# A two-layer decoder on one core: the first self-attention rewritten with four heads side by side on row groups

## The chip, the core and the metric

The kernel runs on one core of a Trainium2 chip. A core has TensorE (PE in the profile, its weight loads PEld), VectorE (DVE), ScalarE (ACT), GpSimd (POOL) and the queue of SyncE (SP), which work side by side and wait for one another by semaphores. Matrix products go from SBUF to PSUM, which has eight banks of 512 float32 columns on 128 partitions; GpSimd works on SBUF alone in this kernel. The metric is the device time of one execution in microseconds. All arrays are float32.

## The reference

Two decoder layers work on x of shape (8, 256, 256): eight batches of 256 tokens, 256 features. Each layer is a self-attention, a cross-attention to a context of 77 tokens and a mixture of experts with two of eight experts per token. Only the self-attention of the first layer is touched here. After a layer norm it computes, with 16 heads of 16 features:

```python
qkv = (x @ W_qkv).reshape(Bx, Nx, 3, H, Dh).transpose(2, 0, 3, 1, 4)
q, k, v = (qkv[0], qkv[1], qkv[2])
allowed = jnp.abs(i - j) <= half          # half = 64, Nx = 256
attn = jnp.einsum('bhqd,bhkd->bhqk', q, k) * scale
attn = jnp.where(allowed[None, None], attn, -jnp.inf)
attn = jax.nn.softmax(attn, axis=-1)
out = jnp.einsum('bhqk,bhkd->bhqd', attn, v)
return out.transpose(0, 2, 1, 3).reshape(Bx, Nx, C) @ W_proj + b_proj
```

The result is added to x. A query sees keys at most 64 places away, so a tile of 128 queries needs 192 of the 256 keys.

## The kernel before

The stages run one after another, with a barrier of all engines between them. The first self-attention is `attention(nc, "L0a", ..., windowed=True)`; its tensors begin with `L0a_`, the cross-attentions' with `L0x_` and `L1x_`, the second self-attention's with `L1a_`, the experts' with `L0f_` and `L1f_`.

One step of this stage is one head j of one batch, 16 steps a batch. The queries of eight heads lie on the 128 partitions, and the keys of a head are kept as a copy of these 128 rows in which the rows of other heads are zero (`k_m`, written by L345, 16 copies a batch). So every product contracts over 128 rows, 16 of which count. For each of the two query tiles q, TensorE makes the scores [128 queries, 192 keys] (L814) and adds the window's mask by a second product in bfloat16 (L817). VectorE takes the negated maximum over the keys (L393), ScalarE writes `prob = exp(s - max)` and the sum of each row (L587), VectorE inverts the sum (L488), GpSimd multiplies `prob` by it (L707), TensorE transposes the normalised `prob` by four products with the identity (L833), and VectorE or ScalarE in turn copies the transposed block out of PSUM (L235, L237). After every fourth head TensorE multiplies by the values (L855): four heads side by side on groups of 32 columns of the array. The projection (L921) follows once a batch, and VectorE adds it to X (L497). The products for queries, keys and values of the next batch (L745, L778) and the transposes of its normalised tokens (L758) are spread over the steps by the table `plan`.

The order on each engine is written out by hand: within `step`, TensorE first turns head j and then makes the scores of head j + 4 (`LOOK`), so four heads are on their way at once; `prob` has four buffers (`NB`), scores and transposed blocks two PSUM banks each. The second self-attention (`attention_quads`, not touched) makes its scores at L1232 with two heads at once, each on 64 rows of the array, into banks of their own.

## Time and profile before

| | us |
|---|---|
| three runs: median (lowest to highest) | 1757.69 (1747.56 to 1760.4) |
| the profiled execution: its time | 1754.57 |
| its span | 1752.9 |
| first self-attention in it, about | 9 to 292 |
| one batch of it | 33.4 |

The profile counts time from the first instruction. The batch of 33.4 us is the distance between two starts of the projection L921. The granted clock of TensorE over the whole execution is 0.956 of full speed, and 1.00 in every window of the first self-attention. The profiled execution is 3.1 us shorter than the median.

### The profile page before, as it was taken

The numbers are of one execution on the slowest core, as the hardware profiler recorded it, in microseconds if no ns is written. First come the engines' busy times: TensorE is split into PE (matmuls) and PEld (weight loads), VectorE is DVE, ScalarE is ACT, GpSimd is POOL, SyncE is SP. The second block draws the span as 40 slices with busy tenths as digits, with TensorE's granted clock in tenths as the row PEclk, the third lists the DMA queues.
The fourth block names the chain that finished last, engine by engine and source line by source line (L and its number), as shares of the span: only waits on it lengthen the run. The fifth ranks groups of instructions, "written<-read, shape, count | busy, mean of one in ns | idle before, by whom it ended". The sixth has DMA issues, their size and how long they took to land. (4 is left out here: it accounts for less than half of the span.)

```text
span 1752.9 us, 37262 instructions
## 1 busy us (share of the span) xinstructions
PE 1576.9 (90%) x10822; PEld 1309.1 (75%) x10823; DVE 824.7 (47%) x2586; ACT 778.5 (44%) x3041; POOL 600.8 (34%) x718
## 2 busy tenths in 40 slices
PE   5999997988749999996999999999688874999997
PEld 4878775766539999995677777776476664999997
DVE  5766664677723333332544444444177762222222
ACT  3665664766512222222445445544176651333333
POOL 3444443455522222221323232323055552222222
PEclk9999999999959999998999999999799986999999
DMA  9800002011113334322000000000301111343331
GB/s 332 261 11 0 0 0 104 29 40 40 37 43 72 93 82 133 74 40 62 1 1 1 1 1 1 1 1 1 111 22 40 40 40 46 86 119 90 95 85 30
DMA packets 81041, 99.32 MB, mean 57 GB/s; under 512 B 10608, under 2 KB 73664, under 8 KB 80960
## 3 DMA queue, kind: packets, MB, share of 16 engines
q1 hardware_dynamic: 65568, 78.61, 14.1%
q0 software_dynamic: 14160, 18.52, 5.8%
q10 hardware_dynamic: 1232, 1.18, 0.2%
q8 instruction: 42, 0.69, 0.2%
q14 instruction: 39, 0.32, 0.1%
HBM read 58.54 MB, written 40.92 MB: 57 GB/s over the span
## 5 line engine op out<-in xcount | busy, mean ns | idle before, releaser
L1176 POOL TENSOR_TENSOR L1a_prob<-L1a_prob,L1a_rtot 128x1024 f32<-128x1024 f32 x64 | 121.1, 1892 | 284.1 <-DVE L1a_rtot L1056 284.1
L1533 PEld LDWEIGHTS L0f_ps_h<-L0f_rows_t,L0f_w_up 128*128 128x128 f32 x1584 | 183.6, 193 | 11.7 <-issue 10.3
L1533 PE MATMUL L0f_ps_h<-L0f_rows_t,L0f_w_up 128*128 128x128 f32 x1584 | 185.2, 277 | 7.1 <-issue 7.1
L1594 ACT ACTIVATE L1f_hid<-L1f_ps_h,L1f_b_up 128x128 f32<-128x128 f32 x296 | 92.4, 363 | 166.0 <-PE L1f_ps_h L1533 166.0
L707 POOL TENSOR_TENSOR L0a_prob<-L0a_prob,L0a_rtot 128x384 f32<-128x384 f32 x128 | 105.4, 826 | 141.6 <-DVE L0a_rtot L488 141.6
L587 ACT ACTIVATE L0a_prob<-L0a_ps_s,L0a_nmax 128x192 f32<-128x192 f32 x256 | 105.5, 418 | 88.9 <-DVE L0a_nmax L393 68.8
L1533 PEld LDWEIGHTS L1f_ps_h<-L1f_rows_t,L1f_w_up 128*128 128x128 f32 x1184 | 139.7, 194 | 3.6 <-issue 1.7
L1533 PE MATMUL L1f_ps_h<-L1f_rows_t,L1f_w_up 128*128 128x128 f32 x1184 | 140.0, 277 | 1.4 <-ACT L1f_rows_t L1570 1.4
L1121 ACT ACTIVATE L1a_prob<-L1a_ps_s,L1a_nmax 128x256 f32<-128x256 f32 x256 | 118.2, 473 | 40.2 <-DVE L1a_nmax L1051 40.2
L1542 PE MATMUL L1f_ps_y<-L1f_w_down,L1f_hid 128*128 128x256 f32 x592 | 133.9, 379 | 0.0
L814 PE MATMUL L0a_ps_s<-L0a_k_m,L0a_q_t 128*128 128x192 f32 x512 | 122.3, 341 | 2.3 <-ACT L0a_prob L587 1.2
L1542 PEld LDWEIGHTS L1f_ps_y<-L1f_w_down,L1f_hid 128*128 128x128 f32 x592 | 109.6, 190 | 13.4
L1582 ACT ACTIVATE L0f_mid<-L0f_ps_h 128x256 f32<-128x256 f32 x72 | 27.6, 384 | 189.9 <-PE L0f_ps_h L1533 180.8
L587 ACT ACTIVATE L1x_prob<-L1x_ps_s,L1x_nmax 128x77 f32<-128x77 f32 x256 | 79.3, 327 | 48.3 <-DVE L1x_nmax L393 41.9
L587 ACT ACTIVATE L0x_prob<-L0x_ps_s,L0x_nmax 128x77 f32<-128x77 f32 x256 | 79.4, 327 | 46.9 <-DVE L0x_nmax L393 31.6
L1542 PE MATMUL L0f_ps_y<-L0f_w_down,L0f_hid 128*128 128x256 f32 x432 | 99.2, 379 | 0.0
L1051 DVE TENSOR_REDUCE L1a_nmax<-L1a_ps_s 128x2 f32<-128x512 f32 x128 | 79.4, 682 | 32.2 <-PE L1a_ps_s L1232 32.1
L1245 PEld LDWEIGHTS L1a_ps_t<-ident,L1a_prob 128*128 128x128 f32 x512 | 61.5, 143 | 40.5 <-issue 31.8
L393 DVE TENSOR_REDUCE L0a_nmax<-L0a_ps_s 128x2 f32<-128x384 f32 x128 | 71.0, 555 | 43.3 <-PE L0a_ps_s L817 36.1
L814 PEld LDWEIGHTS L0a_ps_s<-L0a_k_m,L0a_q_t 128*128 128x128 f32 x512 | 77.1, 190 | 16.6 <-ACT L0a_prob L587 3.9
L1245 PE MATMUL L1a_ps_t<-ident,L1a_prob 128*128 128x128 f32 x512 | 80.5, 281 | 7.9 <-DVE L1a_prob_t L1060 5.5
L1644 DVE TENSOR_TENSOR L0f_hid<-L0f_mid,L0f_ps_h 128x256 f32<-128x256 f32 x72 | 30.3, 421 | 120.1 <-ACT L0f_mid L1582 98.7
(315 smaller groups left out, 3426.6 us busy)
## 6 DMA issues: line engine op xcount, KB each, us to landing
expert_table<-zero SPq DMA_DIRECT2D x1, 16640.0 KB, 65.9
L0f_w_up<-in_w_dram SPq DMA_DIRECT2D x8, 1408.0 KB, 6.2
L1f_w_up<-in_w_dram SPq DMA_DIRECT2D x8, 1024.0 KB, 5.4
L1f_w_down<-in_w_dram SPq DMA_DIRECT2D x8, 1024.0 KB, 7.8
L0f_w_down<-in_w_dram SPq DMA_DIRECT2D x8, 768.0 KB, 8.1
L1f_rows<-expert_table SPq DMA_DIRECT2D x39, 130.0 KB, 2.1
L0f_rows<-expert_table SPq DMA_DIRECT2D x38, 130.0 KB
sums<-X SPq DMA_DIRECT2D x8, 256.0 KB, 2.7
```

The source lines that it names most:

```text
L393: eng.tensor_reduce(nmax[:, j % NB, :], src, AX.X, ALU.max, negate=True).then_inc(max_done, 1)
L587: ins = eng.activation(prob[:, j % NB, r, 0:width], ps_s[:, j % 2, r * width:(r + 1) * width], ACT.Exp, bias=nmax[:, j % NB, r:r + 1], acc ...
L707: eng.tensor_tensor(prob[:, j % NB, :, 0:width], prob[:, j % NB, :, 0:width], rtot[:, j % NB, :].unsqueeze(2).to_broadcast([P, QT_N * G, w ...
L814: ins = eng.matmul(out, q_t[par][:, c, q * P:(q + 1) * P], rhs, start=True, stop=not windowed)
L1051: eng.tensor_reduce(nmax[:, j % RING, :], src, AX.X, ALU.max, negate=True).then_inc(max_done, 1)
L1121: ins = eng.activation(prob[:, j % RING, q, :], ps_s[:, k, q * S:(q + 1) * S], ACT.Exp, bias=nmax[:, j % RING, q:q + 1], accum_out=total[: ...
L1176: eng.tensor_tensor(v, v, r.unsqueeze(2).to_broadcast([P, 2 * QT_N, S]), ALU.mult).then_inc(norm_done, 1)
L1245: ins = eng.transpose(ps_t[:, o:o + P], prob[:, j % RING, q, c * P:(c + 1) * P], ident[:, :])
L1533: ins = eng.matmul(ps_h[:, c, o:o + P], w_up[par][:, t, w0:w0 + P], rows_t[:, t, :], start=(t == 0), stop=(t == DT - 1))
L1542: ins = eng.matmul(ps_y[:, 0:D], hid[:, c, k * P:(k + 1) * P], w_down[par][:, 2 * c + k, :], start=(c == 0 and k == 0), stop=(c == CHUNKS ...
L1594: ins = eng.activation(hid[:, c, k * P:(k + 1) * P], ps_h[:, c, k * P:(k + 1) * P], ACT.Gelu, bias=b_up[par][:, 2 * c + k:2 * c + k + 1])
L1644: ins = eng.tensor_tensor(hid[:, c, :], mid[:, c, :], ps_h[:, c, 2 * P:4 * P], ALU.mult)
```

## The change

The call of `attention` for `L0a` is replaced by a new function, `attention_banded`. The other stages stay as they are; `attention` still serves the two cross-attentions.

A step is now a *unit* u, 32 in all and four a batch: batch b, half c of the heads, and v, the even or the odd heads of that half. The four heads of a unit lie on row groups of 32 partitions (`rows(r)`), 16 rows each, and the other 16 are zero in `q_m`; in `k_m` one of those other rows is -1. `scores` makes the four heads' scores for two query tiles, eight products that contract over 32 rows, each row group into a bank of its own. `maximum` takes the largest masked score of each query with a fused add-and-maximum of VectorE per head and query tile (L1098), 32 a batch, and writes it as a column into `tops`. `turn_tops` transposes these columns, and `shift` adds them to `q_m`, in the row that meets the -1. `turned_scores` then makes the scores again with the keys on the partitions, the maxima already subtracted. ScalarE takes the exponential of a head's 384 columns at once and keeps no sum (L1179). GpSimd sets what is outside the window to zero by `affine_select` (L1208), eight instructions a unit. `values` multiplies by the values and, by a block of ones, gives the sum of each column as well (L1305). VectorE inverts 256 sums per half (L1111) and multiplies (L1117). Normalising before the product, the transposes of `prob` and their copies out of PSUM are gone.

Seven banks of PSUM form one ring. The list `turns` gives every block of scores, maxima, turned scores and projections its turn, and `wait_free` makes a block wait until the block seven turns before has been read.

```diff
@@ -928,6 +928,405 @@
+def attention_banded(nc, name, env, q_scale, wq, wk, wv, wo, bo, x_landed, w_landed, other_loads):
...
+    DH, GROUPS, UNITS = 16, 4, 4
+    W = S - HALF_WINDOW
+    KT = S // P
+    first_key = (0, HALF_WINDOW)
+    BANKS = 7
+    PLAN = [[(1, "k")], [(1, "q")], [(-1, "o")], [(1, "v"), (2, "x")]]
+    FIRST, REST = ["x", "k", "q"], [(0, "v"), (1, "x")]
+    units = B * UNITS
+    def plan(u):
+        return [(u // UNITS + n, e) for n, e in PLAN[u % UNITS] if 0 <= u // UNITS + n < B]
+    def part(u):
+        return u // UNITS, u % UNITS // 2, u % 2
+    turns = [("e", 0, e) for e in FIRST] + [("s", 0, r) for r in range(GROUPS)] + [("e", *e) for e in REST]
+    for u in range(units):
+        if u + 1 < units:
+            turns += [("s", u + 1, r) for r in range(GROUPS)]
+        turns += [("m", u, 0)] + [("e", *e) for e in plan(u)] + [("p", u, r) for r in range(GROUPS)]
+    turns.append(("e", B - 1, "o"))
+    at = {t: i for i, t in enumerate(turns)}
...
+                    eng.memset(v_s[i][:, :, :, :], 0.0).then_inc(cleared, 1)
+                for i in range(UNITS):
+                    eng.memset(tops[i][:, :, :], 0.0).then_inc(cleared, 1)
+                for v in range(2):
+                    other = slice(DH * (1 - v), DH * (1 - v) + 1)
+                    eng.tensor_reduce(mask[:, v:v + 1], env["hmask16"][:, v::2], AX.X, ALU.add).then_inc(built, 1)
+                    eng.tensor_reduce(minus[:, v:v + 1], ident[:, DH * (1 - v)::2 * DH], AX.X, ALU.add, negate=True).then_inc(built, 1)
+                    eng.memset(ones[:, v, :], 0.0).then_inc(built, 1)
+                    eng.wait_ge(built, 4 * v + 3)
+                    eng.memset(ones[:, v, v * DH:(v + 1) * DH], 1.0).then_inc(built, 1)
+                eng.memset(none[:, :], 0.0).then_inc(built, 1)
+                eng.wait_ge(built, 9)
+                eng.tensor_scalar(scale[:, :], mask[:, :], float(q_scale), None, ALU.mult).then_inc(built, 1)
+                eng.tensor_copy(band[:, :, :], env["wmask"][:, :, :]).then_inc(built, 1)
...
+                def take(b, e):
+                    if e == "k":
+                        eng.wait_ge(made, events.index((b, e)) + 1)
+                        for v in range(2):
+                            ins = eng.tensor_scalar(k_m[b % 2][v][:, :, :], bank("e", b, e)[:, :].rearrange("p (c s) -> p c s", c=2),
+                                                    mask[:, v:v + 1], minus[:, v:v + 1], ALU.mult, ALU.add)
+                        ins.then_inc(out_vector, 1)
+                    elif e == "o":
+                        eng.wait_ge(projected, b + 1)
+                        eng.wait_ge(biased, b + 1)
+                        xb = X[:, b * QT_N:(b + 1) * QT_N, :]
+                        eng.tensor_tensor(xb, xb, bank("e", b, e)[:, :].rearrange("p (q d) -> p q d", q=QT_N), ALU.add).then_inc(added, 1)
+                def maximum(u, r):
+                    b, c, v = part(u)
+                    n = u * GROUPS + r
+                    eng.wait_ge(scores_done, n + 1)
+                    at_row = 2 * DH * r + DH * (1 - v)
+                    for q in range(QT_N):
+                        k = n * QT_N + q
+                        if k:
+                            eng.wait_ge(masked_done, k)
+                        ins = eng.tensor_tensor_reduce(masked[:, :], bank("s", u, r)[:, q * W:(q + 1) * W], band[:, q, :], 1.0, -3.0e38,
+                                                       ALU.add, ALU.max, tops[u % UNITS][:, q, at_row:at_row + 1]).then_inc(masked_done, 1)
+                    eng.wait_ge(masked_done, (n + 1) * QT_N)
+                    eng.sem_inc(max_done, 1)
+                def shift(u):
+                    b, c, v = part(u)
+                    eng.wait_ge(tops_turned, u + 1)
+                    q = q_m[b % 2][v][:, c, :]
+                    eng.tensor_tensor(q, q, bank("m", u, 0)[:, 0:S], ALU.add).then_inc(shifted, 1)
+                def sums(b, c):
+                    eng.wait_ge(values_done, 2 * (b * 2 + c + 1))
+                    eng.reciprocal(rsum[:, :], ps_o[:, S:2 * S]).then_inc(rsum_done, 1)
+                def out(b, c):
+                    eng.wait_ge(rsum_done, b * 2 + c + 1)
+                    if c == 0 and b:
+                        eng.wait_ge(projected, b)
+                    eng.tensor_tensor(o_t[:, c, :], ps_o[:, 0:S], rsum[:, :], ALU.mult).then_inc(o_out, 1)
...
+                for e in FIRST:
+                    take(0, e)
+                norm(1, 1)
+                for r in range(GROUPS):
+                    maximum(0, r)
+                for u in range(units):
+                    b, c, v = part(u)
+                    whole = part(u - 2)[:2] if v == 1 and u > 1 else None
+                    if whole:
+                        sums(*whole)
+                    shift(u)
+                    for r in range(GROUPS):
+                        if u + 1 < units:
+                            maximum(u + 1, r)
+                        if whole and r == 1:
+                            out(*whole)
+                    for e in plan(u):
+                        take(*e)
+                    if b + 2 < B and u % UNITS == 1:
+                        norm(b + 2, 0)
+                    if b + 2 < B and u % UNITS == 2:
+                        norm(b + 2, 1)
+                sums(B - 1, 1)
+                out(B - 1, 1)
+                take(B - 1, "o")
...
+                def exponential(u, r):
+                    eng.wait_ge(turned, u * GROUPS + r + 1)
+                    if u >= 2:
+                        eng.wait_ge(values_done, u - 1)
+                    eng.activation(prob[u % 2][:, r, :, :], bank("p", u, r)[:, 0:KT * W].rearrange("p (t w) -> p t w", t=KT),
+                                   ACT.Exp).then_inc(exp_done, 1)
...
+                def window(u, r):
+                    eng.wait_ge(exp_done, u * GROUPS + r + 2)
+                    for t in range(KT):
+                        for sign, cols in ((1, slice(0, HALF_WINDOW * (1 + t))), (-1, slice(HALF_WINDOW * (1 + t), W))):
+                            n = cols.stop - cols.start
+                            p = prob[u % 2][:, r:r + 2, t, cols]
+                            base = HALF_WINDOW * (1 - t) + cols.start if sign == 1 else HALF_WINDOW * (1 + t) - cols.start
+                            ins = eng.affine_select(out=p, in_=p, compare_op=ALU.is_ge, fill=0.0, base=base,
+                                                    pattern=[[0, 2], [sign, n]], channel_multiplier=-sign)
+                    ins.then_inc(banded, 1)
...
+                def rows(r):
+                    return slice(2 * DH * r, 2 * DH * (r + 1))
+                def scores(u):
+                    b, c, v = part(u)
+                    wait_out(eng, b, "q")
+                    wait_out(eng, b, "k")
+                    for r in range(GROUPS):
+                        wait_free(eng, "s", u, r)
+                    for q in range(QT_N):
+                        for r in range(GROUPS):
+                            ins = eng.matmul(bank("s", u, r)[:, q * W:(q + 1) * W], q_m[b % 2][v][rows(r), c, q * P:(q + 1) * P],
+                                             k_m[b % 2][v][rows(r), c, first_key[q]:first_key[q] + W], start=True, stop=True)
+                            if q == QT_N - 1:
+                                ins.then_inc(scores_done, 1)
+                def turn_tops(u):
+                    wait_free(eng, "m", u, 0)
+                    eng.wait_ge(max_done, (u + 1) * GROUPS)
+                    for q in range(QT_N):
+                        ins = eng.transpose(bank("m", u, 0)[:, q * P:(q + 1) * P], tops[u % UNITS][:, q, :], ident[:, :])
+                    ins.then_inc(tops_turned, 1)
+                def turned_scores(u):
+                    b, c, v = part(u)
+                    eng.wait_ge(shifted, u + 1)
+                    for r in range(GROUPS):
+                        wait_free(eng, "p", u, r)
+                    for t in range(KT):
+                        for r in range(GROUPS):
+                            ins = eng.matmul(bank("p", u, r)[:, t * W:(t + 1) * W], k_m[b % 2][v][rows(r), c, t * P:(t + 1) * P],
+                                             q_m[b % 2][v][rows(r), c, first_key[t]:first_key[t] + W], start=True, stop=True)
+                            if t == KT - 1:
+                                ins.then_inc(turned, 1)
+                def values(u):
+                    b, c, v = part(u)
+                    eng.wait_ge(banded, (u + 1) * GROUPS // 2)
+                    if v == 0:
+                        wait_out(eng, b, "v")
+                        if u:
+                            eng.wait_ge(o_out, u // 2)
+                    for summed in range(2):
+                        for t in range(KT):
+                            for r in range(GROUPS):
+                                o = summed * S + first_key[t]
+                                lhs = ones[:, v, :] if summed else v_s[b % 2][:, t, c * 8 + 2 * r + v, :]
+                                ins = eng.matmul(ps_o[rows(r), o:o + W], lhs, prob[u % 2][:, r, t, :], start=(v == 0 and not summed and t == 0),
+                                                 stop=(v == 1 and t == KT - 1), skip_group_check=True)
+                    ins.then_inc(values_done, 1)
+                for e in FIRST:
+                    make(0, e)
+                scores(0)
+                for e in REST:
+                    make(*e)
+                for u in range(units):
+                    if u + 1 < units:
+                        scores(u + 1)
+                    turn_tops(u)
+                    for e in plan(u):
+                        make(*e)
+                    turned_scores(u)
+                    if u:
+                        values(u - 1)
+                values(units - 1)
+                make(B - 1, "o")
...
@@ -1824,8 +2223,8 @@
         routes = [dict(wr=wr, taken=t, experts=numbers[:, 0:EXPERTS], before=before, ones=ones, from_end=from_end,
                        table=table, zero=zero, zeroed=((zeroed, 16),), sums=sums, kept=k)
                   for wr, t, sums, k in ((wr0, taken[0], sums0, kept[0]), (wr1, taken[1], a["out"].rearrange("b s d -> (b s) d"), kept[1]))]
-        attention(nc, "L0a", env, dh=16, windowed=True, q_scale=16 ** -0.5, wq=wq0, wk=wk0, wv=wv0, wo=wo0, bo=bo0,
-                  x_landed=((x_first, 16), (x_rest, 16)), w_landed=((w0_landed, W0),), other_loads=later_loads)
+        attention_banded(nc, "L0a", env, 16 ** -0.5, wq0, wk0, wv0, wo0, bo0, ((x_first, 16), (x_rest, 16)),
+                         ((w0_landed, W0),), later_loads)
         with nc.Block() as block:
             @block.scalar
             def _(eng):
```

On TensorE, the steady part of a batch. Before, one head stood like this (L833 turns a head, L814 and L817 make the scores of another, L855 are the values of four heads; the `REGISTER_ALU` rows count semaphores):

```order
L823 REGISTER_ALU
L833 MATMUL L0a_ps_t<-ident,L0a_prob 128x128 x4
L803 REGISTER_ALU
L814 MATMUL L0a_ps_s<-L0a_k_m,L0a_q_t 128x192
L817 MATMUL L0a_ps_s<-wmask,identb 128x192
L814 MATMUL L0a_ps_s<-L0a_k_m,L0a_q_t 128x192
L817 MATMUL L0a_ps_s<-wmask,identb 128x192
L855 MATMUL L0a_ps_o<-L0a_prob_t,L0a_v_s 32x256 x8
L833 MATMUL L0a_ps_t<-ident,L0a_prob 128x128 x4
```

After the change, one unit of four heads stands like this (L1278 turns the maxima, L1288 makes the turned scores, L1305 values and sums, L1269 the next unit's scores; the names of the waits are the semaphores):

```order
L1278 MATMUL L0a_ps<-ident,L0a_tops 128x128 [waits L0a_max,L0a_exp]
L1278 MATMUL L0a_ps<-ident,L0a_tops 128x128
L1288 MATMUL L0a_ps<-L0a_q_m,L0a_k_m 128x192 [waits L0a_max,L0a_exp,L0a_shifted]
L1288 MATMUL L0a_ps<-L0a_q_m,L0a_k_m 128x192 x7
L1305 MATMUL L0a_ps_o<-L0a_prob,L0a_v_s 32x192 [waits L0a_banded]
L1305 MATMUL L0a_ps_o<-L0a_prob,L0a_v_s 32x192 x7
L1305 MATMUL L0a_ps_o<-L0a_prob,L0a_ones 32x192 x8
L1269 MATMUL L0a_ps<-L0a_k_m,L0a_q_m 128x192 [waits L0a_max,L0a_shifted,L0a_exp,L0a_out_vector,L0a_out_scalar]
L1269 MATMUL L0a_ps<-L0a_k_m,L0a_q_m 128x192 x7
```

A unit is now four blocks for four heads (2, 8, 16 and 8 products), and the scores L1269 stand between one unit's values L1305 and the turning of the maxima, which stands before the next L1288.

On VectorE, before, two heads of the steady part (L488 inverts a head's sums, L393 takes a maximum, L345 masks keys, L235 copies a transposed block):

```order
L488 RECIPROCAL L0a_rtot<-L0a_total 128x2
L389 REGISTER_ALU
L393 TENSOR_REDUCE L0a_nmax<-L0a_ps_s 128x2
L345 TENSOR_TENSOR L0a_k_m<-L0a_ps_k,hmask 128x512
L488 RECIPROCAL L0a_rtot<-L0a_total 128x2
L235 COPY L0a_prob_t<-L0a_ps_t 128x512
L389 REGISTER_ALU
L393 TENSOR_REDUCE L0a_nmax<-L0a_ps_s 128x2
L345 TENSOR_TENSOR L0a_k_m<-L0a_ps_k,hmask 128x512
L488 RECIPROCAL L0a_rtot<-L0a_total 128x2
```

After the change, from the inversion of a half's sums on (`ISA` rows of L1098 come in pairs, the fused maximum and the reading of its accumulator; L1107 is `shift`):

```order
L1111 RECIPROCAL L0a_rsum<-L0a_ps_o 128x256 [waits L0a_values]
L1107 TENSOR_TENSOR L0a_q_m<-L0a_q_m,L0a_ps 128x256 [waits L0a_tops_turned]
L1098 ISA L0a_masked,L0a_tops<-L0a_ps,L0a_band 128x192 [waits L0a_masked,L0a_scores]
L1098 ISA L0a_tops 128x1
L1098 ISA L0a_masked,L0a_tops<-L0a_ps,L0a_band 128x192 [waits L0a_masked]
L1098 ISA L0a_tops 128x1
L1098 ISA L0a_masked,L0a_tops<-L0a_ps,L0a_band 128x192 [waits L0a_masked,L0a_scores]
L1098 ISA L0a_tops 128x1
L1098 ISA L0a_masked,L0a_tops<-L0a_ps,L0a_band 128x192 [waits L0a_masked]
L1098 ISA L0a_tops 128x1
L1117 TENSOR_TENSOR L0a_o_t<-L0a_ps_o,L0a_rsum 128x256 [waits L0a_masked,L0a_rsum]
L1098 ISA L0a_masked,L0a_tops<-L0a_ps,L0a_band 128x192 [waits L0a_masked,L0a_scores]
```

The inversion of 128x256 sums stands in front of `shift`, `shift` in front of the next unit's eight maxima, and every maximum waits for the one before it (`L0a_masked`), because all write their masked scores into the same buffer.

## Rows read from the trace of the kernel before

**Rows 1.** The page: busy time of each engine, share of the span, instructions

```profile
PE 1576.9 (90%) x10822; PEld 1309.1 (75%) x10823; DVE 824.7 (47%) x2586; ACT 778.5 (44%) x3041; POOL 600.8 (34%) x718
```

**Rows 2.** Busy time by window: PE, PEld, DVE, ACT, POOL, then clock, DMA

```profile
123.60:157.00 33.40, 33.40 (x264) 26.63 (x260) 22.37 (x56) 20.38 (x78) 15.23 (x19) 1.00 0.00 0
257.00:292.00 35.00, 32.23 (x274) 24.15 (x262) 17.70 (x45) 19.68 (x77) 15.19 (x18) 1.00 0.01 1
```

**Rows 3.** Waits from 60 to 280 us: total us, times, longest

```profile
DVE L0a_nmax L393 <- PE L0a_ps_s L817: 28.0, 46, 1.8
```

**Rows 4.** Groups by form, 0 to 400 us: xcount | busy us, mean ns | idle before

```profile
L814 PE MATMUL L0a_ps_s<-L0a_k_m,L0a_q_t 128*128 128x192 f32 x512 | 122.3, 341 | 2.3 <-ACT L0a_prob L587 1.2 <-issue 1.2
...
L817 PE MATMUL L0a_ps_s<-wmask,identb 128*128 128x192 bf16 x256 | 63.0, 246 | 0.0
...
L833 PE MATMUL L0a_ps_t<-ident,L0a_prob 128*128 128x128 f32 x512 | 78.2, 275 | 0.2 <-ACT L0a_prob_t L237 0.2
```

**Rows 5.** Timeline of PE in one batch: start us, us, instruction, xcount

```profile
122.72 1.07 PE L855 MATMUL L0a_ps_o<-L0a_prob_t,L0a_v_s 128*32 128x256 f32 x16
...
123.72 0.66 PE L833 MATMUL L0a_ps_t<-ident,L0a_prob 128*128 128x128 f32 x4
```

**Rows 6.** Timeline of PE in the second self-attention (L1a)

```profile
969.96 1.89 PE L1218 MATMUL L1a_ps_f<-L1a_xt,wq 128*128 128x256 f32 x8
...
971.69 0.60 PE L1245 MATMUL L1a_ps_t<-ident,L1a_prob 128*128 128x128 f32 x4
...
973.94 2.00 PE L1232 MATMUL L1a_ps_s<-L1a_k_t,L1a_q_t 64*128 64x256 f32 x16
...
975.86 0.44 PE L1261 MATMUL L1a_ps_o<-L1a_prob_t,L1a_v_s 128*64 128x256 f32 x2
```

**Rows 7.** Groups by form, DVE, 0 to 400 us

```profile
L497 DVE TENSOR_TENSOR X<-X,L0a_ps_o 128x512 f32 x6 | 4.1, 687 | 3.9 <-PE L0a_ps_o L921 3.9
...
L369 DVE TENSOR_TENSOR L0x_v_s<-L0x_ps_k,bv 77x256 f32<-77x256 f32 x5 | 2.1, 421 | 2.4 <-PE L0x_ps_k L795 2.4
...
L488 DVE RECIPROCAL L0a_rtot<-L0a_total 128x2 f32<-128x2 f32 x128 | 19.7, 154 | 1.2 <-ACT L0a_prob L587 1.2
```

**Rows 8.** Groups by form, second self-attention, 860 to 1120 us

```profile
L1056 DVE RECIPROCAL L1a_rtot<-L1a_total 128x4 f32<-128x4 f32 x40 | 6.8, 170 | 11.8 <-ACT L1a_prob L1121 11.8
...
L1121 ACT ACTIVATE L1a_prob<-L1a_ps_s,L1a_nmax 128x256 f32<-128x256 f32 x164 | 75.7, 473 | 23.6 <-DVE L1a_nmax L1051 23.6
```

**Rows 9.** Timeline of DVE where each instruction waits for the one before

```profile
372.89 0.17 DVE L474 TENSOR_TENSOR taken<-L0x_counts,taken 128x8 f32<-128x8 f32 x1
373.09 0.17 DVE L473 TENSOR_TENSOR L0x_place<-L0x_counts,taken 128x8 f32<-128x8 f32 x1
```

**Rows 10.** Busy time by window again, clock behind POOL

```profile
468.00:470.00 2.00, 0.76 (x7) 0.79 (x8) 1.75 (x4) 1.20 (x9) 1.80 (x3) 1.00 0.00 0
1402.00:1404.00 2.00, 1.09 (x8) 0.86 (x8) 2.00 (x6) 0.69 (x5) 1.24 (x3) 1.00 0.00 0
1404.00:1406.00 2.00, 1.77 (x13) 1.39 (x14) 1.27 (x8) 1.81 (x8) 1.14 (x3) 0.76 0.36 124
1406.00:1408.00 2.00, 2.00 (x6) 1.53 (x6) 1.52 (x3) 1.33 (x8) 1.83 (x3) 0.50 0.22 74
1408.00:1410.00 2.00, 2.00 (x15) 1.85 (x14) 0.56 (x1) 0.60 (x1) 0.33 (x1) 0.88 0.19 67
```

**Rows 11.** Timeline at the start and the end of the stage

```profile
11.89 0.73 DVE L318 TENSOR_SCALAR L0a_xn<-X,L0a_mv,L0a_rstd 128x256 f32<-128x256 f32 x2 [1.11 <-POOL L0a_rstd L658]
...
12.75 0.72 PEld L758 LDWEIGHTS L0a_ps_f<-ident,L0a_xn 128*128 128x128 f32 x4 [12.43 <-DMA bo<-in_bo_dram]
...
18.50 4.88 DVE L345 TENSOR_TENSOR L0a_k_m<-L0a_ps_k,hmask 128x512 f32<-128x512 f32 x8 [1.03 <-PE L0a_ps_k L745]
...
290.88 0.69 DVE L497 TENSOR_TENSOR X<-X,L0a_ps_o 128x512 f32<-128x512 f32 x1 [3.74 <-PE L0a_ps_o L921]
```

**Rows 12.** Timeline of POOL at the start

```profile
1.28 0.28 POOL L1747 TENSOR_SCALAR_AFFINE_SELECT ident<-ident 128x128 f32<-128x128 f32 x1 [0.24 <-POOL ident L1746]
```

## What the change will do to the time

> **What bounds the kernel now.** I read the page first, then windows of the first self-attention, its waits, and last its groups and timelines by instruction. The page shows TensorE busy 90% of the span, VectorE 47% [rows 1]. In a batch of the stage that changes, TensorE is busy all 33.4 us at full clock, while VectorE works 22.4, ScalarE 20.4 and GpSimd 15.2 us [rows 2]. The largest wait of VectorE there is for TensorE's scores: 28 us in 220, 46 times [rows 3]. So TensorE's order of work sets the stage, eight batches from about 24 us on, and its last instruction ends at 290.88 + 0.69 = 291.6 us [rows 11]. Everything after it starts behind a barrier, so what this stage gains or loses moves the end by as much.
>
> **What goes from TensorE, what comes.** Gone are L814, L817 and L833 (122, 63 and 78 us of busy time, overlapping) [rows 4]. For the new blocks I take distances from start to start.
> - A full-array product over 256 columns costs 0.432: four in 971.69 - 969.96 = 1.73 [rows 6]; 192 columns 0.324.
> - Eight products over two row groups (L1232) take 975.86 - 973.94 = 1.92 [rows 6], that is four steps of 0.432 and 0.19 of overhead, so two row groups work at once. If four do, `scores` and `turned_scores` are two steps of 0.324 + 0.19 = 0.84 each.
> - `values` and its sums: four column groups work at once already (L855, two steps of 0.432 in 123.72 - 122.72 = 1.00 [rows 5]); now four steps of 0.324 + 0.19 = 1.49.
> - `turn_tops`: L833's four transposes end after 0.66 [rows 5] and follow each other by 0.11, two end after 0.44.
>
> With projections (four of 1.73, one of 0.44), a batch needs 4 x (0.84 + 1.49 + 0.84 + 0.27) + 7.4 = 21.1 us of TensorE in place of 33.4. It is no longer the bound; the question is what is.
>
> **VectorE's maxima.** The fused maximum has no row. A tensor operation on PSUM costs 0.421 for 256 and 0.687 for 512 columns [rows 7], so 0.155 + 1.04 ns per column: 0.355 for 192. Behind it comes a reading of the accumulator, of the size of a small operation (0.15, rows 9). Instructions without a wait overlap by 0.07 (the eight L345 at the start take 4.88 us in a row, 0.61 each [rows 11], where one of 512 columns lasts 0.687 [rows 7]); one that waits for the one before starts 0.03 after its end (0.17 long, 0.20 apart [rows 9]). I take 0.46 for a maximum, and 0.99 for the two of a head, with 0.07 for the instruction that tells TensorE. Bounds: reading hidden, 0.39 and 0.80; nothing overlapped and the wait paid twice, 0.62 and 1.30. I take the value nearest to the small operations. [...]
>
> **The inversion.** L1111 inverts 256 sums at once. The rows invert 2 in 0.154 [rows 7] and 4 in 0.170 us [rows 8], 8 ns per column where L369 and L497 show 1.04. By that slope 256 cost 2.2 us; if it were like a product, 0.42. I take 2.2, because the two rows are the same operation, though 16 ns is a thin base. The Trainium skill (VectorE: DVE Perf Modes, "The DVE is not a fixed-function vector unit", the hardware budget) says that the reciprocal is an iterated division with a repeat count of 8; by it the sum would be 2.1 + 0.155, by the product rows 14 us less over the stage.
>
> **The new circle.** The ring of seven banks ties the units together. `turned_scores(u)` needs the bank of `scores(u+1)`'s third head, so it waits until VectorE has done three heads of maxima of u+1. Then TensorE does turned scores, `values(u-1)`, `scores(u+2)` and only then `turn_tops(u+1)`; VectorE's `shift(u+1)` waits for that, and stands in front of the maxima of u+2. One round:
> 0.13 (VectorE to TensorE: L318 ends at 12.62, the load of weights begins at 12.75 [rows 11]) + 0.84 + 1.49 + 0.84 + 0.47 (turned, with 0.03 to VectorE) + 0.35 (shift, 0.421 less overlap) + 3 x 0.99 = 7.09 us. Four are 28.4. The product L1117 stands between the maxima in two of four, + 0.70. The unit with two projections pushes the ring by one, and its turned scores wait for the fourth head, + 0.99.
> While TensorE has its 3.77 us of the round, VectorE has the fourth head (0.99) and what `plan` gives it: masked keys 1.3 and the inversion 2.2 in one round, addition 0.69, normalising 0.7 and the inversion in another. That is 4.49 and 4.58: late by 1.5 together. The batch: 28.4 + 0.7 + 1.0 + 1.5 = **31.6 us**, 1.8 less than 33.4.
> ScalarE costs nothing: 256 columns take 0.473 with their sum [rows 8], so 384 some 0.58; a unit 2.3 of 7.9 us, and only the first head's exponential is needed by `scores(u+2)`, 1.49 us later. GpSimd neither: 0.28 for a select of 128 columns [rows 12], some 0.4 for 256, 2.8 us per unit, done about 5 us after the turned scores, before `values` asks a round later. If that cover went (1.7 times as long), the batch would grow by 2 us.
>
> **Start and end.** VectorE begins with 5.1 us of clearing and masks (1.8 in two memsets, the rest in some fifteen small operations) before the first layer norm, then the old way to the first scores, then four heads of maxima: `shift(0)` at about 31.5. Thirty-one rounds are 7.75 batches: 245, so `shift(31)` at 276.5. Behind it turned scores 1, exponentials 2.3, selects 1.5, values 1.6, inversion 2.2, product 0.4, projection 2.1, addition 0.7: 12.5. The stage would end at 289, 2.6 before now: 1754.6 - 2.6 = 1752 us at full clock. (The profiled execution is 3.1 below the median of 1757.7; I leave the numbers on its basis.)
>
> **The clock.** TensorE now waits in every round: 7.1 less 3.64 and a projection of 1.73 leave 1.9 us, and in the rounds with a late VectorE or a fourth head about 3. In the trace the clock stayed at full speed behind 2 us with 0.76 busy, 468 to 470 [rows 10]; but it fell to its lower level (2.4 to 1.2 GHz) behind 1402 to 1404, with 1.09 busy, and over three windows 0.24 + 0.50 + 0.12 of 2 us were lost, 1.7 us [rows 10]. So two rounds of four stand where it fell. Each costs 1.7, of which the late VectorE hides some: 1.5 x 2 x 8 = 24 us. The Trainium skill (TensorE: Matmul & The Clock Gate, "A second HAM failure mode: psum-queue depth-cycling") tells of a kernel whose idle moments between groups of products, one per turn of its PSUM banks, let the clock swing between its levels. By it the case with dips holds, without it the 1752.
>
> **Forecast and rivals.**
> - Forecast, 35%: inversion slow, clock falls twice a batch: 1752 + 24 = **1776**; its own range 1760 to 1792.
> - The clock holds, 25%: 1752. For it speaks the stretch at 468.
> - Faster, 22%: inversion like a product and 0.80 a head. The round is 6.52, nothing is late: 26.1 + 0.7 + 0.8 = 27.6 a batch, 31 less in 7.75, 3 less at the ends, waits of TensorE of 1.3 us and a full clock: 1718.
> - Slower by the maxima, 14%: each 0.1 us a head adds 12 us to the ring (three per round and the fourth), so from 1.19 on it alone passes 1775. At 1.30, four rounds + 3.7, the fourth heads + 0.9: 4.65 x 7.75 = 36 and 2 at the start: 1790, with the dips 1814. For it speaks that every maximum waits for the one before; against it the 0.03 [rows 9].
> - The row groups don't work side by side, so the change doesn't do what it says, 4%: each block of scores is eight steps, 2.78 for 0.84, 3.9 more a round: + 120, 1872 or more. Against it, L1232.
>
> **The numbers.** What can be told from no change is 1%, 17.6 us: below 1740 faster, above 1775 slower. Faster: 20 of the 22 and 5 of the second case, 25%. Slower: half of the forecast's 35, 3 of the second case, and the last two, 38%. Same: 37%. The range leaves out the lower third of the fast case and the upper half of the maxima's with the last: 1716 to 1816.
>
> **What would show it.** L1098 with its reading about 0.46 apart (0.39: the fast case; 0.62: the slow one). L1111 at 2.2 or 0.42 us. L1269 and L1288 about 0.84 from start to next block; 2.8 would mean one after another. PEclk below 1.0 in the slices of 40 to 280 us. `turned_scores` waiting for VectorE's maxima, `shift` for L1278. A wait of L1305 for GpSimd would prove the cover wrong. I am wrong altogether if another engine than VectorE and TensorE in turn ends the waits.

## The result, and the profile after

The changed kernel takes 1763.3 us (median of 20 runs, 1757.5 to 1770.2), the kernel before 1757.2 (20 runs): a ratio of 1.0040, 95% interval 1.0025 to 1.0054. The change costs 0.4%, about 7 us by the ratio (the medians lie 6.2 apart). The forecast was 1776 us, with 1716 to 1816 as the range. One run of the kernel before took 1919.4 us and doesn't count in the ratio.

The page of the changed kernel, first section and row of the granted clock (40 slices of 44 us; the kernel before had no slice below 9 in the first six):

```profile
PE 1511.3 (86%) x11142; PEld 1237.5 (70%) x11143; DVE 812.3 (46%) x2797; ACT 691.2 (39%) x2585; POOL 575.2 (33%) x846
...
PEclk9899987899959999998999999999699996999999
```

TensorE is busy 65.6 us less than the 1576.9 of before [rows 1], and the kernel didn't gain. The stage's last instruction shows where it stands:

```profile
299.58 0.69 DVE L1087 TENSOR_TENSOR X<-X,L0a_ps 128x512 f32<-128x512 f32 x1 [3.94 <-PE L0a_ps L1248]
```

The stage ends at 300.27 us, before it was 291.6 [rows 11]: 8.7 us more. What lies behind takes 1463.1 us of the span of 1763.4, and took 1461.3 of 1752.9. So most of the difference of the two profiled executions (10.5 us) lies in the stage.

Waits between 60 and 280 us (total us, times, longest):

```profile
POOL L0a_prob L1208 <- ACT L0a_prob L1179: 142.9, 27, 7.4
ACT L0a_prob L1179 <- PE L0a_ps L1288: 122.3, 27, 7.6
PEld L0a_ps L1288 <- issue: 62.5, 26, 3.2
DVE L0a_q_m L1107 <- PE L0a_ps L1278: 58.3, 14, 6.8
PE L0a_ps L1288 <- DVEq L1101: 56.8, 27, 3.0
```

Before, TensorE waited for hardly anything and VectorE for its scores [rows 2, 3]. Now TensorE's turned scores (L1288) wait 27 times for the instruction that tells of the maxima (L1101, in VectorE's queue), and VectorE's `shift` waits for TensorE's L1278: the two take turns.

One such turn, TensorE and VectorE (start us, us, instruction; for merged rows the start of the first):

```profile
180.70 0.42 DVE L1107 TENSOR_TENSOR L0a_q_m<-L0a_q_m,L0a_ps 128x256 f32<-128x256 f32 x1 [3.17 <-PE L0a_ps L1278]
181.04 0.35 DVE L1098 CUSTOM_DVE_ANT_0 L0a_masked<-L0a_ps,L0a_band 128x192 f32<-128x192 f32 x1
181.32 0.08 DVE L1098 DVE_READ_ACCUMULATOR2_ANT L0a_tops<- 128x1 f32 x1
181.44 0.36 DVE L1098 CUSTOM_DVE_ANT_0 L0a_masked<-L0a_ps,L0a_band 128x192 f32<-128x192 f32 x1
181.72 0.08 DVE L1098 DVE_READ_ACCUMULATOR2_ANT L0a_tops<- 128x1 f32 x1
182.07 0.36 DVE L1098 CUSTOM_DVE_ANT_0 L0a_masked<-L0a_ps,L0a_band 128x192 f32<-128x192 f32 x1 [0.27 <-DVE L0a_tops L1098]
...
184.07 0.93 PE L1288 MATMUL L0a_ps<-L0a_q_m,L0a_k_m 32*128 32x192 f32 x16 [1.68 <-DVEq L1101]
...
184.93 0.86 PE L1305 MATMUL L0a_ps_o<-L0a_prob,L0a_v_s 128*32 128x192 f32 x16
...
186.37 0.93 PE L1269 MATMUL L0a_ps<-L0a_k_m,L0a_q_m 32*128 32x192 f32 x16
186.51 1.76 DVE L1111 RECIPROCAL L0a_rsum<-L0a_ps_o 128x256 f32<-128x256 f32 x1
...
187.23 0.44 PE L1278 MATMUL L0a_ps<-ident,L0a_tops 128*128 128x128 f32 x2
...
188.18 0.36 DVE L1107 TENSOR_TENSOR L0a_q_m<-L0a_q_m,L0a_ps 128x256 f32<-128x256 f32 x1
```

From block to block TensorE needs 0.86, 1.44 and 0.86 us: the four row groups do run side by side. A head's maxima lie 0.40 apart, and the next head's first one 0.63 behind the second: 1.03 us a head. The inversion begins when the values are done and ends 0.6 us behind L1278; `shift` starts only at its end, 0.5 us behind L1278: this round lasts 188.18 - 180.70 = 7.48 us.

And the rounds one after another, each from `shift` to `shift` (busy time of PE, PEld, DVE, ACT, POOL with counts, then granted clock, DMA):

```profile
188.18:198.03 9.85, 6.88 (x77) 4.70 (x76) 3.53 (x20) 2.80 (x7) 3.72 (x11) 0.83 0.00 0
198.03:205.50 7.47, 5.39 (x75) 3.88 (x74) 6.37 (x20) 1.64 (x4) 2.58 (x9) 1.00 0.01 2
205.50:212.73 7.23, 5.33 (x75) 3.85 (x74) 4.59 (x23) 3.09 (x6) 2.00 (x7) 1.00 0.00 0
212.73:220.21 7.48, 5.80 (x78) 4.25 (x77) 6.27 (x21) 1.64 (x4) 3.79 (x12) 1.00 0.01 3
220.21:231.41 11.20, 8.23 (x77) 5.63 (x76) 3.52 (x19) 2.79 (x7) 4.05 (x11) 0.70 0.01 1
```

The first six batches have each one round of 9.7 to 11.2 us, the one with two projections, where the granted clock falls (1.2 GHz in part of it), and half of the batches have one more of 8.8. Neither what such a round would take at full clock nor why it falls can be read here. That is the first thing to try.

### The profile page after: what moved, and what is told of

Same layout as the page of the kernel before. It is cut to its first block and busy times, and to the rows that moved or that the text cites. A ratio compares the mean times of both kernels' runs of the same rounds, so it can differ in the third digit from the quotient of the medians.

```text
span 1763.4 us, 37023 instructions
## 1 busy us (share of the span) xinstructions
PE 1511.3 (86%) x11142; PEld 1237.5 (70%) x11143; DVE 812.3 (46%) x2797; ACT 691.2 (39%) x2585; POOL 575.2 (33%) x846
## 5 line engine op out<-in xcount | busy, mean ns | idle before, releaser
L1208 POOL TENSOR_SCALAR_AFFINE_SELECT L0a_prob<-L0a_prob 128x128 f32<-128x128 f32 (+1 forms) x256 | 79.7, 351 | 178.2 <-ACT L0a_prob L1179 178.2
L1941 PEld LDWEIGHTS L1f_ps_y<-L1f_w_down,L1f_hid 128*128 128x128 f32 x592 | 109.6, 190 | 13.4
L1179 ACT ACTIVATE L0a_prob<-L0a_ps 128x384 f32<-128x384 f32 x128 | 52.5, 498 | 142.5 <-PE L0a_ps L1288 142.5
L1098 DVE CUSTOM_DVE_ANT_0 L0a_masked<-L0a_ps,L0a_band 128x192 f32<-128x192 f32 x256 | 91.1, 356 | 28.3 <-DVE L0a_tops L1098 21.9
L1288 PE MATMUL L0a_ps<-L0a_q_m,L0a_k_m 32*128 32x192 f32 x512 | 33.1, 374 | 64.4 <-DVEq L1101 62.5
L1941 PEld LDWEIGHTS L0f_ps_y<-L0f_w_down,L0f_hid 128*128 128x128 f32 x432 | 79.3, 190 | 9.3
```

The costliest lines, as they stand in the source:

```text
L1098: ins = eng.tensor_tensor_reduce(masked[:, :], bank("s", u, r)[:, q * W:(q + 1) * W], band[:, q, :], 1.0, -3.0e38, ALU.add, ALU.max, tops[ ...
L1179: eng.activation(prob[u % 2][:, r, :, :], bank("p", u, r)[:, 0:KT * W].rearrange("p (t w) -> p t w", t=KT), ACT.Exp).then_inc(exp_done, 1)
L1208: ins = eng.affine_select(out=p, in_=p, compare_op=ALU.is_ge, fill=0.0, base=base, pattern=[[0, 2], [sign, n]], channel_multiplier=-sign)
L1288: ins = eng.matmul(bank("p", u, r)[:, t * W:(t + 1) * W], k_m[b % 2][v][rows(r), c, t * P:(t + 1) * P], q_m[b % 2][v][rows(r), c, first_ke ...
L1941: ins = eng.matmul(ps_y[:, 0:D], hid[:, c, k * P:(k + 1) * P], w_down[par][:, 2 * c + k, :], start=(c == 0 and k == 0), stop=(c == CHUNKS ...
```

## The experiments

All times are medians (20 runs of the changed kernel, 10 of `inv_two_columns`, 4 or 5 of the others); the ratio is to the kernel before, run on the same chip. "Stage end" is the end of the last instruction of the first self-attention in the profile (291.6 before, 300.3 after the change); "batch" is four consecutive rounds, from one `shift` to the fourth behind it, at full clock. An edit can move the lines behind it by a few, so that L1248 of the changed kernel is L1249 or L1241 in another.

| kernel | us | ratio (95%) | stage end | batch |
|---|---|---|---|---|
| change | 1763.3 | 1.0040 (1.0025 to 1.0054) | 300.3 | 30.5 (seen in `fill`) |
| fill | 1740.3 | 0.9902 (0.9887 to 0.9916) | 279.4 | 30.5 |
| inv_two_columns | 1760.1 | 1.0017 (1.0001 to 1.0032) | 287.7 | - |
| told | 1746.4 | 0.9937 (0.9920 to 0.9954) | 279.0 | 28.7 |
| four_masked | 1746.3 | 0.9933 (0.9912 to 0.9955) | 279.8 | 28.8 |
| told_four | 1707.8 | 0.9729 (0.9694 to 0.9765) | 237.7 | 25.5 |
| bank_order | 1791.3 | 1.0202 (1.0183 to 1.0220) | 326.0 | - |
| reorder | 1739.9 | 0.9897 (0.9875 to 0.9920) | 268.6 | 28.5 |
| ts_first | 1716.5 | 0.9759 (0.9735 to 0.9783) | 258.1 | 27.3 |
| best1 | 1705.2 | 0.9704 (0.9687 to 0.9721) | 234.9 | 25.3 |
| best2 | 1731.3 | 0.9863 (0.9831 to 0.9894) | 260.2 | 28.3 |
| best3 | 1695.2 | 0.9651 (0.9620 to 0.9682) | 224.0 | 24.3 |

Stage ends tell the edits apart better than times: what lies behind the stage took 1461 to 1470 us in these profiles, with the same instructions. Why it varies I did not look into. And a profile is of one execution, which need not lie at the median: that of `ts_first` took 1728.2 us (the slowest of its four, median 1716.5), that of `best1` 1698.3 (the fastest, median 1705.2).

### Fill: TensorE's waits filled

```
 def turned_scores(u):
     b, c, v = part(u)
+    wait_free(eng, "p", u, 0)
+    for q in range(3):
+        eng.matmul(bank("p", u, 0)[:, 0:2 * P], ident[:, :], wq[:, 0, :], start=True, stop=True)
     eng.wait_ge(shifted, u + 1)
```

> Added to the changed kernel: in front of each unit's turned scores TensorE makes three products of the identity and 256 weight columns (about 1.3 us) into the bank that the turned scores overwrite, in time in which it waited for the maxima; the results don't change. Theory: the half-speed stretches of TensorE cost the stage what its rounds are longer by than undisturbed ones of the same place in the batch, some 19 us in the 31 rounds of the profile (8.8, 9.8 and 11.2 us where 7.2 and 8.3 stand without). With the waits filled the granted clock stays at 1.00 from 60 to 280 us, the rounds become 7.5, 7.2, 7.5 and 8.3, the stage ends about 19 us earlier, and the time is 1740 to 1748 us. Rival: the clock falls all the same, since the waits that matter are those behind the values and in front of the scores, and the time stays within 4 us of 1763. Second rival: the clock holds, but the added products stand in the way of the turned scores where VectorE is early, and the rounds grow by 0.3 us each: 1752 to 1757.

Measured: 1740.3 us, 23 less than the changed kernel, with 96 products more (192 instructions in the trace). Four rounds by window:

```profile
146.75:155.02 8.27, 6.60 (x83) 4.99 (x82) 3.53 (x20) 2.79 (x7) 2.14 (x8) 1.00 0.01 2
155.02:162.50 7.48, 6.70 (x81) 5.02 (x80) 6.38 (x21) 1.64 (x4) 4.17 (x12) 1.00 0.00 0
162.50:169.72 7.22, 6.62 (x81) 4.99 (x80) 4.58 (x23) 3.08 (x6) 1.99 (x7) 1.00 0.01 3
169.72:177.20 7.48, 7.10 (x84) 5.39 (x83) 6.27 (x21) 1.64 (x4) 3.79 (x12) 1.00 0.01 3
```

VectorE's columns are those of the changed kernel (3.53, 6.37, 4.59, 6.27), the short rounds are as long as there, and the long ones are 8.27 for 9.85 and 11.20. From 60 to 260 us the granted clock is 1.00. The stage ends 20.9 us earlier: the 31 rounds together are 22.4 us shorter, the first `shift` comes 1.0 later, and what follows the last takes 0.45 more. So the clock costs the changed kernel about 21 us, and the change without it would end its stage 12.2 us before 291.6. (The very last projection runs at half speed in both, 3.75 us, and so do parts of the start; that is not in the 21.) This also gives the clean batch: 7.48 + 7.22 + 7.48 + 8.27 = 30.45 us. The last of these rounds stands at full clock in `inv_two_columns` too, which has no idle products: 8.33 us, twice.

### The inversion on two columns

```
+    eng.memset(rsum[:, :], 1.0).then_inc(cleared, 1)
...
-    eng.reciprocal(rsum[:, :], ps_o[:, S:2 * S])
+    eng.reciprocal(rsum[:, 0:2], ps_o[:, S:S + 2])
```

The kernel leaves out the inversion of the other 254 columns, which stay at the 1.0 written once at the start.

> The changed kernel, but of the 256 columns of sums only 2 are inverted (the output is scaled wrongly): the 1.76 us instruction becomes one of about 0.15. Theory, from the rounds of the changed kernel: the inversion starts 0.07 us behind the values and ends just when or 0.5 us after the transposed maxima do. In the round with the addition the shift then comes 0.48 us earlier (7.48 to 7.0); in the one with the masked keys TensorE is late by itself (7.44), because its scores wait for the keys. So 0.5 us a batch and 1.6 at the end, 5 to 6 us less than the changed kernel: 1757 to 1758. Rival, the prediction's: VectorE is late by 0.75 in both rounds: 12 us and 1.6, about 1750. Rival that the stage is bound by VectorE's whole work: 16 times 1.6, 25 us less, 1738.

Measured: 1760.1 us, 3 less. The inversion lasts 0.17 instead of 1.76 us. The round with the addition falls from 7.48 to 7.00 as the theory said, the one with the masked keys stays at 7.48. The stage ends 12.6 us earlier, more than the theory's 5 to 6: six rounds with the addition give 2.7, the last round 1.3 and the last inversion 1.6. The other 7 us come mostly from half-speed stretches that fell elsewhere, 1.8 of them in the last projection:

```profile
295.79 3.75 PE L1248 MATMUL L0a_ps<-wo,L0a_o_t 128*128 128x256 f32 x8 [2.41 <-DVE L0a_o_t L1117]
```

```profile
284.98 1.97 PE L1249 MATMUL L0a_ps<-wo,L0a_o_t 128*128 128x256 f32 x8 [0.84 <-DVE L0a_o_t L1118]
```

The first line is the changed kernel, the second this one. Behind the stage 3.3 us are given back. The two rivals (1750, 1738) are out: the inversion's length is nearly all hidden.

Why the round with the masked keys stays at 7.48 the changed kernel shows:

```profile
202.38 1.53 DVE L1080 TENSOR_SCALAR L0a_k_m<-L0a_ps,L0a_mask,L0a_minus 128x512 f32<-128x512 f32 x2 [0.16 <-DVE L0a_tops L1098]
202.93 0.83 PE L1305 MATMUL L0a_ps_o<-L0a_prob,L0a_ones 128*32 128x192 f32 x16
...
204.16 0.93 PE L1269 MATMUL L0a_ps<-L0a_k_m,L0a_q_m 32*128 32x192 f32 x16 [0.40 <-ACT L0a_prob L1179]
```

By `turns`, the third head of the next scores takes the bank from which VectorE reads the keys (L1080), and the scores start 0.25 us behind the end of that reading, 0.40 behind the values. The profile puts the wait down to ScalarE, whose last exponential ends at about the same time; the code has the scores wait only for the first one, long done.

### The maxima: told by their own count, four buffers, and both

`told` (the wait and the separate count behind a head go; TensorE waits for the maxima's own semaphore):

```
-    eng.wait_ge(masked_done, (n + 1) * QT_N)
-    eng.sem_inc(max_done, 1)
...
-    eng.wait_ge(max_done, (u + 1) * GROUPS)
+    eng.wait_ge(masked_done, (u + 1) * GROUPS * QT_N)
```

> The changed kernel, but TensorE is told of a head's maxima by the semaphore that each maximum already counts, so that the wait and the separate count behind every head are gone. Theory: between the two maxima of a head 0.40 us lie from start to start, between heads 0.63; the 0.23 more are the two semaphore instructions of VectorE's queue. Gone, a head costs 0.80; three heads of each round and the fourth of one in four are on the ring: 13 x 0.23 = 3.0 us a batch, about 23 us in the stage, 1738 to 1742 us. Rival: half of the gap is the wait for the head's scores, which stays: 0.12 a head, 1750 to 1752. Second rival: the ring is shorter but the clock falls more often, within 4 us of 1763.

Measured: 1746.4, between the theory (1738 to 1742) and the rival (1750 to 1752). A head takes 0.92 us, not 0.80: the distance to the next head falls from 0.63 to 0.51, the rival's half of the gap. `four_masked`:

```
-    if k:
-        eng.wait_ge(masked_done, k)
-    ins = eng.tensor_tensor_reduce(masked[:, :], ...
+    if k >= 4:
+        eng.wait_ge(masked_done, k - 3)
+    ins = eng.tensor_tensor_reduce(masked[k % 4][:, :], ...
```

> The changed kernel with four buffers for the masked scores, so that a maximum waits for the fourth before it and not for the one before it (TensorE is told as in the changed kernel). Theory: the wait costs nothing, since the reading of the accumulator (0.08 us) follows the maximum on the same engine in any case and the next one can't start before it; the pitch in a head stays at 0.40, a head at 1.03, the time within 3 us of 1763. Rival: the wait is the 0.12 us between the start of the reading and the start of the next maximum; without it the pitch is 0.32 to 0.36, a head 0.90 to 0.95, and 13 of those a batch give 8 to 13 us less.

Measured: 1746.3. My theory fell: the wait for the maximum before does cost 0.12 us, the distance inside a head falls from 0.40 to 0.28, and the 17 us are more than even the rival's 8 to 13. Both together, `told_four`:

> The changed kernel with both edits of the maxima: four buffers for the masked scores, and TensorE told by the maxima's own count. With one of them alone a head took 0.92 us (1.03 without), and with four buffers the second maximum of a head started 0.28 us behind the first, while its accumulator was read. Theory: the two savings add, since one is inside a head and the other between heads: 0.28 and about 0.42, 0.70 a head; a batch falls from 30.5 to 26 to 27 us, and with one or two half-speed stretches a batch the time is 1732 to 1740. Rival: between heads the semaphore instruction that waits for the head's scores sets the distance, and a head stays at 0.9: 1746.

Measured: 1707.8 us, 55.5 less than the changed kernel where the two edits alone gave 17 each. VectorE of `told_four`:

```profile
93.74 0.35 DVE L1098 CUSTOM_DVE_ANT_0 L0a_masked<-L0a_ps,L0a_band 128x192 f32<-128x192 f32 x1
94.01 0.08 DVE L1098 DVE_READ_ACCUMULATOR2_ANT L0a_tops<- 128x1 f32 x1
94.01 0.35 DVE L1098 CUSTOM_DVE_ANT_0 L0a_masked<-L0a_ps,L0a_band 128x192 f32<-128x192 f32 x1
94.29 0.08 DVE L1098 DVE_READ_ACCUMULATOR2_ANT L0a_tops<- 128x1 f32 x1
94.29 0.35 DVE L1098 CUSTOM_DVE_ANT_0 L0a_masked<-L0a_ps,L0a_band 128x192 f32<-128x192 f32 x1
...
95.63 0.93 PE L1286 MATMUL L0a_ps<-L0a_q_m,L0a_k_m 32*128 32x192 f32 x16 [0.54 <-DVE L0a_tops L1098]
```

The maxima follow each other by 0.28 us, inside a head and between heads: 0.56 a head, less than the theory's 0.70. With either edit alone, VectorE still waits between two maxima of every head for the one just before. In `told_four` two waits still stand between two heads, for the next head's scores and for the maximum four before; both were met in time and cost nothing to be seen. So what `told` left, 0.51 for 0.40, was not the wait for the scores alone, as its rival had it. TensorE's wait for the maxima is 0.54 us in this round instead of 1.68. The batch is 4.9 us shorter than 30.45, 38 us in 7.75 batches, and from 60 to 230 us the clock no longer falls (1.00), which is most of the rest of 62.5 us.

### Bank_order: only the banks dealt differently

```
 for u in range(units):
+    turns += [("e", *e) for e in plan(u)]
     if u + 1 < units:
         turns += [("s", u + 1, r) for r in range(GROUPS)]
-    turns += [("m", u, 0)] + [("e", *e) for e in plan(u)] + [("p", u, r) for r in range(GROUPS)]
+    turns += [("m", u, 0)] + [("p", u, r) for r in range(GROUPS)]
```

> The changed kernel with no instruction moved: only the numbers of the banks are dealt out differently (a unit's projections take theirs ahead of the next unit's scores), so that the turned scores wait for the second head's maxima and not for the third's, and in the unit with two projections also for the second and not the fourth. Theory: the ring of banks binds in the rounds without an inversion at their end: they go from 7.23 and 8.27 to about 6.2 each, while the two with an inversion stay at 7.48, because there VectorE's own work (four heads, masked keys or addition and normalising, inversion) is as long. 3.1 us a batch, 24 us in the stage before the clock; TensorE then waits in fewer and longer pieces, which may cost some us: 1737 to 1745. Rival: VectorE's work binds all rounds, and the wait for the bank is only its shadow: within 4 us of 1763.

Measured: 1791.3, 28 us more; both theories missed. TensorE and VectorE of one round:

```profile
195.84 1.89 PE L1249 MATMUL L0a_ps<-wo,L0a_o_t 128*128 128x256 f32 x8
201.45 1.08 PE L1289 MATMUL L0a_ps<-L0a_q_m,L0a_k_m 32*128 32x192 f32 x16 [3.73 <-issue]
```

And VectorE in the same round:

```profile
200.46 0.69 DVE L1088 TENSOR_TENSOR X<-X,L0a_ps 128x512 f32<-128x512 f32 x1 [0.23 <-DVE L0a_tops L1099]
```

The turned scores now get the bank of the projection made just before, and VectorE takes that out (L1088) only behind all eight maxima: they start 0.30 us behind its end, 5.4 us into the round and not at 3.4; behind the masked keys at 6.1. My theory had asked which scores' bank they need, and not who holds the others. The two such rounds of a batch take 11 to 12.5 us, and in this one the clock fell behind the wait of 3.7 us: the values (L1306) start 1.28 us apart, and not 0.68. The stage ends 25.7 us later than the changed kernel's, nearly all of the 28. That one renumbering does this shows that the ring of banks binds here.

### Reorder and ts_first: TensorE's blocks in another order

`reorder`, with the banks in the same order:

```
 for u in range(units):
+    turn_tops(u)
     if u + 1 < units:
         scores(u + 1)
-    turn_tops(u)
     for e in plan(u):
         make(*e)
-    turned_scores(u)
     if u:
         values(u - 1)
+    turned_scores(u)
```

> The changed kernel with the order of TensorE's blocks (and so of the seven banks) turned: transposed maxima of a unit, then scores of the next, projection, values of the unit before, turned scores last. The turned scores then need banks freed by the first heads' maxima and not by the third's. Theory: the circle turned scores, values, scores, transposed maxima, shift behind the third head breaks up, and VectorE's own work sets the batch: four times (0.42 shift, 4.15 maxima, 0.5 waiting for the scores) and 3.3, 1.25, 3.3, 0.65 of other work or waits and 0.44 of products, 29.2 us for 30.5, 10 us less in the stage, and 5 to 15 us more because TensorE waits less in one piece and its clock falls less often: 1738 to 1753. Rival: a new wait (turned scores for the exponentials' banks, or the selects in front of the values) takes its place, and the time is 1763 or more.

Measured: 1739.9, a batch of 8.69 + 5.57 + 8.56 + 5.64 = 28.5 us. TensorE shows the new wait:

```profile
107.20 0.44 PE L1279 MATMUL L0a_ps<-ident,L0a_tops 128*128 128x128 f32 x2
108.30 0.93 PE L1270 MATMUL L0a_ps<-L0a_k_m,L0a_q_m 32*128 32x192 f32 x16 [0.67 <-ACT L0a_prob L1180]
```

The scores wait 0.67 us for ScalarE's exponentials: the rival's wait, but smaller than what the order gains. From 60 to 230 us the clock stays at 1.00; the batch accounts for 15 of the 31.7 us by which the stage is shorter than the changed kernel's, and the clock for most of the rest. `ts_first` moves `turned_scores(u)` ahead of `values(u - 1)`:

> The kernel with the turned order of TensorE's blocks (transposed maxima, scores, projection, values, turned scores), but with the turned scores in front of the values. Theory: there every other round lost 0.7 us in front of the scores, from the end of the transposed maxima to the start of the scores, because the scores need a bank that ScalarE's second exponential must have read; with the turned scores 1.4 us earlier that wait is gone, twice a batch, and the wait of VectorE for its scores goes from 1.55 to 0.9 us behind the shift: 1.3 us a batch, 10 us less than the turned order, about 1730. Rival: the turned scores now wait for the second head's maxima instead, and push the values and the transposed maxima back by as much: within 3 us of 1740.

Measured: 1716.5. The batch is 27.3 us as expected (28.5 - 1.3); the stage ends 10.5 us earlier. The medians lie 23 us apart, but the two profiled executions only 12.2: the profile of `ts_first` is of its slowest run, and what made the others faster no trace here shows.

### Three combinations

`best1` is `ts_first` and `told`, and

```
+                    shift(u)
                     if whole:
                         sums(*whole)
-                    shift(u)
...
-                        if whole and r == 1:
+                        if whole and r == 0:
                             out(*whole)
...
+                    elif e == "k":
+                        for v in range(2):
+                            ins = eng.activation(k_m[b % 2][v][:, :, :], src, ACT.Identity, bias=minus[:, v:v + 1], scale=mask[:, v:v + 1])
```

The last cut is in ScalarE's `take`; VectorE's own lines for the keys are gone.

> As the one with turned scores in front of the values, and with the masked keys on ScalarE (two instructions of about 0.8 us, for two of the same on VectorE), TensorE told of the maxima by their own count, and the inversion behind the shift, where VectorE waits for scores, with the product behind the first head's maxima. Theory: VectorE's work in a batch is 4 x 0.42 + 16 x 0.92 + 3.5 + 0.85 + 0.7 + 0.8 + 1.25 = 23.5 us, TensorE's 22; some waits remain between them, so 25 us a batch where the turned order took 28.5: 27 us less than 1740, 1713. Rival: TensorE's and VectorE's work still stand in one chain (transposed maxima, shift, scores, maxima) and the batch stays above 27.5 us, above 1730. Second rival: the product comes too late for the values, which stand in front of the transposed maxima: as long as the first rival.

Measured: 1705.2, with a batch of 25.3 us where the theory had 25 and 1713. `best2` adds the four buffers and deals the projections' banks ahead of the scores':

> The fastest so far (turned order, turned scores ahead of the values, masked keys on ScalarE, inversion behind the shift) with four buffers for the masked scores, and the banks dealt so that the turned scores need the first head's maxima alone. Theory: a batch had rounds of 5.46, 6.64, 5.70 and 7.53 us. Turned scores then start when the projection is done (2.6 us) instead of behind two or four heads; TensorE's blocks alone make 5.4 a round and 7.1 in the one with two projections, so a batch is 22.5 to 23.5 us and the stage 15 to 20 us shorter: 1684 to 1692. Rival: in the rounds with an inversion VectorE stays at 6.6 us whatever TensorE does, and the exponential of the third head, whose bank the next scores now take, adds a wait of 0.3 a round: 24.5 us or more, 1700.

Measured: 1731.3, 26 slower than `best1`: what `bank_order` showed. TensorE's turned scores (L1281) wait, from 60 to 250 us:

```profile
PE L0a_ps L1281 <- ACT L0a_k_m L1160: 10.5, 6, 1.8
...
PE L0a_ps L1281 <- DVE X L1079: 9.0, 7, 1.4
```

In the rounds without an inversion they start 4.0 to 4.6 us behind `shift`, where `best1` has them at 2.7: with the keys after ScalarE's taking out, with the addition after VectorE's, as in `bank_order`. `best3` is `best1` with four buffers and its own banks:

> The kernel with turned order, turned scores ahead of the values, masked keys on ScalarE, inversion behind the shift and TensorE told by the maxima's count, now with four buffers for the masked scores, and with its banks dealt as there: a unit's projections behind its scores, so that the turned scores wait for the second head's maxima (the fourth's in the unit with two projections) and never for a projection that is still to be taken out. Theory: rounds of 5.46, 6.64, 5.70 and 7.53 us become 5.4, 6.3, 5.4 and 7.1, TensorE's own blocks in three of them and VectorE's inversion in one: 24.2 us a batch, 8 to 9 us less in the stage than 234.9, 1694 to 1698. Rival: the turned scores wait for ScalarE's taking out here as well, as in the kernel whose projections come ahead of the scores: rounds of 7 us and 1720 or more.

Measured: 1695.2 us, 3.5% less than the kernel before. A batch of it (columns as above):

```profile
100.62:124.87 24.25, 22.39 (x304) 15.95 (x304) 16.80 (x79) 10.48 (x23) 11.94 (x36) 1.00 0.08 19
```

TensorE is busy 22.4 of 24.3 us at full clock: it is the bound once more, as in [rows 2], with a batch 9 us shorter than there.

## Why the prediction was wrong

The time lies in the range, but the forecast was 12.7 us too high: +18 where +7 came. The step that failed is a term of the sum, the clean batch: 31.6 us forecast, 30.45 measured. The mechanism was right in the main; sizes were off, nearly all in one direction, and one of the two late rounds had another cause than the forecast gave it.

- **What bounds.** Right: TensorE and VectorE take turns through seven banks, L1288 waits for the maxima, `shift` for L1278. GpSimd and ScalarE stay hidden, but for 2.0 us of L1305 at the very end.
- **Blocks.** 0.84, 1.49 and 0.84 forecast, 0.86, 1.44 and 0.86 measured.
- **A head of maxima.** 0.99 forecast, 1.03 measured, by luck in its parts: 0.40 between the two and not 0.46, but 0.63 to the next head and not 0.53. Of that `told` takes 0.12 away by leaving out the wait and the count. I priced the wait of one maximum for the other at 0.03 from TENSOR_TENSORs in a chain [rows 9]; `four_masked` shows 0.12, the distance falling from 0.40 to 0.28. The Trainium skill (VectorE: DVE Perf Modes, "The DRAIN you can't avoid") reports eight copies that took as long with a semaphore after each as with one after the last, and says that a next instruction which is not held starts earlier. The second agrees, the maxima start 0.28 apart at a recorded 0.35; the first doesn't hold here, where a wait for the maximum just before costs 0.12.
- **The inversion.** 2.2 forecast from two tiny rows 8 ns a column apart, 1.76 measured. With the 0.17 for 2 columns that is 6.2 ns a column, where the slope of the two tiny rows gave 8. Two rounds of a batch are late by 0.47 us each, 0.94 and not 1.5. Only in the one with the addition is it the inversion: `inv_two_columns` takes the 0.47 away there and leaves the round with the masked keys at 7.48, because that one waits for the bank of the keys, a wait that the forecast didn't have.
- **The clean batch, the step that failed.** 31.6 forecast, 30.45 measured in `fill`: ring 4 x 7.01 = 28.0 for 28.4 (7.01 is the round with the addition in `inv_two_columns`, at full clock and free of the long inversion), the product L1117 0.44 for 0.70, the fourth head 1.04 for 0.99, the late VectorE 0.94 for 1.5. That is 1.15 in each of 7.75 batches, 9 us. The last batch, which makes nothing for a next one, has rounds of 6.1 to 7.5 us in `fill`; I took it for a full one, some 3 us more. The first `shift` came at 31.85 (31.5 forecast), the end of the stage 13.5 us behind the last `shift`. 12.5 was forecast, but the terms given there add up to 11.8; 1.8 us of what is missing is the last projection at half speed, 3.75 us for 1.97.
- **The clock.** 24 us forecast, 21 measured, by luck in the parts: 16 losses of 1.5 us were forecast, in the rounds with a late VectorE or a fourth head. Set against `fill`, 12 rounds are longer by more than 1 us, ten of them by 1.5 to 1.6 and two by 2.7 and 2.9. The rounds late by 0.47 lost nothing, each is as long as in `fill`; what lost were the six rounds with two projections, three of those with the product for the queries, and three at the very end. (The wait worked out for an ordinary round, 7.1 less 3.64 and 1.73, is 1.7 and not 1.9; the changed kernel shows 1.68.) The Trainium skill (TensorE: Matmul & The Clock Gate, "A second HAM failure mode: psum-queue depth-cycling") describes such a case in bfloat16, and the trace agrees for float32: waits inside every turn of the banks, a clock that swings, 23 us back when they are filled.

Together the stage was to end at 313 us and ended at 300.3, the 12.7 us of the forecast. The sum put a gain of 2.6 us against a loss of 24; measured, a gain of 12.2 stands against a loss of 20.9. The batch was 4% too long and the clock's term 15% too high, but the gain is the small difference of two batches (33.4 less 31.6, and less 30.45), and so it was forecast at a fifth of its size.

## What to carry to other kernels

Work taken from the bounding engine buys little while the engines then take turns over a ring of banks (TensorE's work in a batch fell from 33.4 us to some 22, as in `best3`, and the batch at full clock only to 30.45): first look who frees the bank that the next block asks for, and how late that reader comes in its queue. A TensorE that waits a few us in every round may pay for its waits twice, by the clock, and idle products into a bank that is overwritten anyway show in one run how much. Small waits between short instructions on the chain (a shared scratch buffer, a separate count) are worth more than they look once they come 256 times, and two of them can hide each other's gain: 17 us each alone, 55 together.

## What the runs showed of the hardware that I had not expected

- A fused add and maximum over 128x192 lasts 0.356 us and the reading of its accumulator 0.083, but with four scratch buffers and no other wait they follow each other every 0.28 us; with one buffer every 0.40.
- A wait for the maximum just before puts 0.12 us between two maxima; the separate wait and count behind a head, 0.12 more to the next head (0.63 for 0.51) while the single buffer stays. Waits that were met long before cost nothing to be seen (`told_four`, 0.28 between heads too).
- An inversion of 128x256 takes 1.76 us and one of 128x2 0.17: 6.2 ns a column, against the 1.04 of other operations on PSUM [rows 7].
